# Graph convolution of a graph network in products of rounded halves, with the counts rounded once and at most five rows gathered for their rest

## The reference

```python
def _gcn_conv(x, src, dst, W, b, n):
    h = x @ W
    deg = jax.ops.segment_sum(jnp.ones_like(dst, dtype=x.dtype), dst, num_segments=n)
    dis = jnp.where(deg > 0, jax.lax.rsqrt(jnp.maximum(deg, 1.0)), 0.0)
    norm = dis[src] * dis[dst]
    msg = h[src] * norm[:, None]
    out = jax.ops.segment_sum(msg, dst, num_segments=n)
    return out + b

x = x + blocks(relu(layernorm(x)), ...)          # the four blocks
h = jnp.maximum(_layernorm(x, axis=-1), 0.0)
h = relu(_gcn_conv(h, src, dst, W1, b1, n))      # with one more loop on each node
x = x + _gcn_conv(h, src, dst, W2, b2, n)
```

## Time and profile before

| | |
|---|---|
| median of 3 runs | 1967.62 us (1966.53 to 1967.95) |
| the profiled execution | 1967.23 us |
| its span, first to last instruction | 1965.5 us |
| PE busy | 1890.2 us, 96% of the span |
| DVE, ACT, POOL busy | 1373.7, 783.1, 449.4 us |
| mean granted TensorE clock | 0.994 of full speed |

### The profile page before, as it was taken

One profiled execution on the slowest core, in us unless ns is written; L12 is line 12 of the kernel. 1 busy time (PEld: TensorE's weight loads), 2 busy tenths in 40 slices (PEclk: granted clock), 3 DMA queues, 4 the chain that ended last, 5 costly groups with the idle time before them and its releaser, 6 DMA issues. The chain is left out here.

```text
span 1965.5 us, 33581 instructions
## 1 busy us (share of the span) xinstructions
PE 1890.2 (96%) x11664; PEld 1562.3 (79%) x11664; DVE 1373.7 (70%) x2830; ACT 783.1 (40%) x1528; POOL 449.4 (23%) x525
## 2 busy tenths in 40 slices
PE   6988999999999999999999999999999999899999
PEld 3545888999889899988898999889989998775443
DVE  7887658888875588888657888885498888730111
ACT  1332455555432355544224555542255554330000
POOL 1000243112342422213325111252241113500000
PEclk9999999999999999999999999999999999999999
DMA  4112553111300112112102110301121106110001
GB/s 136 47 43 44 154 160 105 37 37 29 117 33 22 58 39 63 34 39 83 40 25 66 54 36 25 121 1 43 48 58 37 36 26 177 42 37 0 0 21 31
DMA packets 50719, 108.36 MB, mean 55 GB/s; under 512 B 18143, under 2 KB 18195, under 8 KB 50608
## 3 DMA queue, kind: packets, MB, share of 16 engines
q1 hardware_dynamic: 50608, 106.87, 18.5%
HBM read 83.60 MB, written 23.25 MB: 54 GB/s over the span
## 5 line engine op out<-in xcount | busy, mean ns | idle before, releaser
L785 ACT ACTIVATE PT<-ps 125x500 fp32r<-125x500 f32 (+1 forms) x480 | 214.2, 520 | 324.3 <-PE ps L1596 324.3
L1503 PE MATMUL ps<-PT,V 125*128 125x250 f32 x2400 | 313.2, 284 | 1.6 <-DVE PT L1173 1.6
L1503 PE MATMUL ps<-kT,qg 128*125 128x512 f32 (+1 forms) x1440 | 302.5, 354 | 6.8 <-DVE nmx L1157 5.5
L1503 PEld LDWEIGHTS ps<-PT,V 125*128 125x128 f32 x2400 | 289.6, 190 | 2.9 <-DVE PT L1173 2.9
L1503 PEld LDWEIGHTS ps<-kT,qg 128*125 128x125 f32 x1440 | 246.0, 186 | 57.3 <-issue 9.6
L1173 DVE TENSOR_TENSOR PT<-ps,PT 125x500 fp32r<-125x500 f32 (+1 forms) x480 | 253.0, 582 | 2.1 <-ACT PT L785 1.8
L1157 DVE CUSTOM_DVE_ANT_0 SB<-ps,bt 125x1250 f32<-125x1250 f32 x140 | 203.9, 1457 | 47.0 <-PE ps L1503 44.6
L1596 PE MATMUL ps<-ident,pbuf 125*125 125x125 f32 x1600 | 202.4, 274 | 13.6 <-DVE pbuf L1166 13.6
L1596 PEld LDWEIGHTS ps<-ident,pbuf 125*125 125x125 f32 x1600 | 187.3, 189 | 16.6 <-DVE pbuf L1166 15.9
L779 ACT ACTIVATE pbuf<-SB,nmx 125x1250 f32<-125x1250 f32 x140 | 188.1, 1344 | 8.7 <-DVE nmx L1157 7.4
L1166 DVE TENSOR_SCALAR pbuf<-pbuf,rden 125x1250 f32<-125x1250 f32 x160 | 149.8, 936 | 5.6
(11 more groups left out here) (194 smaller groups left out, 2715.4 us busy)
## 6 DMA issues: line engine op xcount, KB each, us to landing
bt<-edge_bias_scratch SPq DMA_DIRECT2D x40, 546.9 KB
q_scratch<-qc SPq DMA_DIRECT2D x16, 500.0 KB, 2.6
qc<-q_scratch SPq DMA_DIRECT2D x16, 500.0 KB, 4.8
counts_scratch<-cblk SPq DMA_DIRECT2D x10, 546.9 KB
c_rows<-counts_scratch SPq DMA_DIRECT2D x10, 546.9 KB
edge_bias_scratch<-b_rows SPq DMA_DIRECT2D x10, 546.9 KB
counts<-counts_scratch SPq DMA_DIRECT2D x10, 546.9 KB
wm<-in_L_gnn_wo_dram SPq DMA_DIRECT2D x4, 1024.0 KB, 8.4
```

Of the source, the lines that this page charges most:

```text
L785: sc.activation(PT[:, h % 2, 0, a:b, u * T:(u + 1) * T], ps_T[0:T, i, 0:(b - a) * T].rearrange("p (t n) -> p t n", n=T), ACT.Copy).then_in ...
L1503: e = mm(out_, lhs(a), rhs(b), start=start and i == 0, stop=stop and i == 2)
```

## The change

1. The counts of each tile are written once more as float32r (`whole`), in place, by an ACT copy that also sums each row (`whole_out`). The kernel takes whole numbers up to 4096 as exact in it. The rows of W1's product are kept as two halves, `hsH` (ACT, `rows_out`) and `hsL` (DVE, `rows_low`).
2. Both aggregations take two float32r matmuls (`hsH` and `hsL` with `whole`) for one in float32. The W2 product takes three, by `product`: W2 is split into `W2h` (ACT) and `W2l` (DVE), the first aggregation's result into `aggH` (ACT) and `aggL` (DVE).
3. A row of counts whose sum reaches 4096 has a rest that `whole` drops. At most five rows can. Ten small matmuls (`tri`, `ones` with `flag`) number them, a selection matrix `sel` is built, ten matmuls read their row numbers, POOL gathers these rows of the counts from DRAM by an indirect DMA, their rest `rest5` is computed on DVE, and one matmul of 5 rows per output piece adds it (`add_rest`, `last_rest`). This always runs, whatever the counts.
4. x is added by POOL ahead of the MLP bias for chunks 2 to 4, and by DVE for chunks 0 and 1, after `front_mod` in chunks 2 and 3. `front_relu(0)` moves on DVE from the last MLP chunk to the one before it. POOL adds the self loops and writes `diags`. The first four `whole_out` stand in ACT's order in the last two MLP chunks, the other six in the last stage.
5. The spread of `dis` (ones with `diags`) is done after the third chunk of the last stage.

The core of the diff:

```diff
@@ gpsimd, layer and what follows it
                     if c + 1 < NC:
+                        if last and c:
+                            add_x(c + 1)
                         mlp_bias(l, c + 1)
-                    if last and c in (1, 2):
-                        add_x(c - 1)
+                    if last and c >= 2:
+                        for t in (2 * c - 4, 2 * c - 3):
+                            self_loop(t)
...
-            for c in range(2, NC):
-                add_x(c)
+            pool.wait_ge(s["wa"], AHEAD + 3 * L + 1)
             g.memset(ones[:, :], 1.0).then_inc(s["onesr"], 1)
...
+            for t in range(NT):
+                e = g.tensor_scalar(diags[:, t * T:(t + 1) * T], ident[0:T, 0:T], dis[:, t:t + 1], None, ALU.mult)
...
+            for t in range(6, NT):
+                self_loop(t)
+            pool.wait_ge(s["g_wide"], 5)
+            g.indirect_dma_start(wide_x[:, :], None, counts_dram[:, :],
+                                 bass.IndirectOffsetOnAxis(ap=idx[:, 0:1], axis=0)).then_inc(s["g_gath"], 16)
@@ scalar
+            def whole_out(t):
+                act.wait_ge(s["g_eye"], t + 1)
+                sc.activation(whole[t][:, :], counts[t][:, :], ACT.Copy, accum_out=hsum[:, t:t + 1]).then_inc(s["g_H"], 1)
...
                     for c in range(NC):
                         if c:
                             yT_out(f2 + c)
-                        rsqrt0(f2 + c + 1)
-                        if c == NC - 1:
+                        if c < NC - 1:
+                            rsqrt0(f2 + c + 1)
+                        else:
                             front_relu(0)
                         h_out(l, c)
...
+                        if c == NC - 2:
+                            rsqrt0(f2 + NC)
+                        if c >= NC - 2:
+                            for t in range(2 * c - 6, 2 * c - 4):
+                                whole_out(t)
...
                 for u in range(2):
-                    act.wait_ge(s["g_hs_mm"], 2 * c + u + 1)
-                    sc.activation(hs[:, 2 * c + u, :], ps_q[0:T, u, :], ACT.Copy, scale=dis[:, 2 * c + u:2 * c + u + 1]).then_inc(s["g_hs"], 1)
+                    rows_out(2 * c + u, u, 2 * c + u)
+                if c == 0:
+                    for t in (4, 5):
+                        whole_out(t)
+                else:
+                    whole_out(5 + c)
+                if c == 1:
...
+                    sc.activation(W2h[:, :, :], W2[:, :, :], ACT.Copy).then_inc(s["g_w2h"], 1)
@@ vector
                     front_mod(f2 + c + 1)
+                    if last and c in (2, 3):
+                        add_x(c - 2)
+                    if last and c == 3:
+                        front_relu(0)
                     mlp_add(l, c, yT, weights)
 
                 dve.wait_ge(s["zC"], AHEAD + f + 2 * (NC - 1))
                 if last:
-                    front_relu(0)
                     front_relu(1)
...
-                yT_low(fg + c, yT2 if c % 2 else yT)
+                yT_low(fg + c, yTb if c % 2 else yT)
+                for u in range(2):
+                    rows_low(2 * (c - 1) + u, u, 2 * (c - 1) + u)
@@ tensor
-            for j in range(KD):
...
-                    for m in range(NT):
-                        e = mm(psf[:, o + a:o + b], hs[:, m, j * 128:(j + 1) * 128], counts[m][:, a:b],
-                               start=(m == 0), stop=(m == NT - 1))
+            def gather_rows(j, p):
...
+                for m in range(NT):
+                    if j == 0 and p == 0:
+                        pe.wait_ge(s["g_H"], m + 1)
+                        pe.wait_ge(s["g_hs"], m + 1)
+                    for i, half in enumerate((hsH, hsL)):
+                        mm(psf[:, o + a:o + b], half[:, m, j * 128:(j + 1) * 128], whole[m][:, a:b], start=m == 0 and i == 0,
+                           stop=False, skip_group_check=True)
+            pe.wait_ge(s["g_disb"], 1)
+            gather_rows(0, 0)
...
+            gather_rows(0, 1)
...
+            gather_rows(0, 2)
+            wide_rows(6)
...
+            pe.wait_ge(s["g_b5"], 2)
+            gather_rows(1, 0)
+            gather_rows(1, 1)
+            pe.wait_ge(s["g_h5e"], 1)
+            pe.wait_ge(s["g_b5"], 5)
+            for p in range(3):
+                add_rest(0, p)
...
-                    e = mm(ps_q[0:T, t % 2, :], aggT[:, k, t * T:(t + 1) * T], W2[:, k, :], start=(k == 0), stop=(k == KD - 1))
+                    e = product(ps_q[0:T, t % 2, :], lambda i: (aggH, aggL)[i][:, k, t * T:(t + 1) * T],
+                                lambda i: (W2h, W2l)[i][:, k, :], k == 0, k == KD - 1)
...
-                for m in range(NT):
-                    e = mm(ps[0:T, t % 2, :], counts[m][:, t * T:(t + 1) * T], hs[:, m, :], start=(m == 0), stop=(m == NT - 1))
+            last_rows(0)
+            wide_rows(2)
+            last_rows(1)
```

More of the change, by code:

```diff
@@ L180, in build @@
-        hs = place("hs", [T, NT, D], F32, r_wm)
+        r_counts = ([r_kv + 4 * KD * D + 5024 * i for i in range(3)] + [r_kv + 4 * 8 * KD * D + 5024 * i for i in range(3)]
+                    + [r_kv + 4 * 3 * KD * D + 5024 * i for i in range(4)])
+        assert r_counts[2] + 4 * N <= r_kv + 4 * 3 * KD * D and r_counts[5] + 4 * N <= kv_end
+        counts = [place(f"counts{t}", [T, N], F32, r_counts[t]) for t in range(NT)]
+        whole = [place(f"whole{t}", [T, N], F32R, r_counts[t]) for t in range(NT)]
@@ new lines, in _ @@
+            dve.wait_ge(s["g_wide"], 2)
+            dve.wait_ge(s["g_wide"], 1)
+            for r in range(WIDE):
+                e = v.scalar_tensor_tensor(out=sel[:, :, r], in0=ps[0:T, 6, 0:NT], scalar=float(r), in1=flag[:, :],
+                                           op0=ALU.is_equal, op1=ALU.mult)
+            e.then_inc(s["g_wide"], 1)
+            dve.wait_ge(s["g_wide"], 4)
+            v.tensor_copy(idx[:, :], ps[0:WIDE, 7, 0:1]).then_inc(s["g_wide"], 1)
+            dve.wait_ge(s["g_h5"], 1)
@@ new lines, in add_rest, with wide_rows @@
+            def add_rest(j, p):
+                a, b = COLS[p]
+                o = 1536 * (j % 2)
+                mm(psf[:, o + a:o + b], hs5[0][:, j * 128:(j + 1) * 128], rest5[:, a:b], start=False, stop=True,
+                   skip_group_check=True).then_inc(s["g_ag"], 1)
+            def wide_rows(bank):
+                for m in range(NT):
+                    e = mm(ps[0:WIDE, bank, :], sel[:, m, :], hsH[:, m, :], start=m == 0, stop=m == NT - 1)
+                e.then_inc(s["g_h5"], 1)
@@ new lines, in _ @@
+            pe.wait_ge(s["g_disb"], 1)
+            gather_rows(0, 0)
+            pe.wait_ge(s["g_tri"], 2)
+            pe.wait_ge(s["g_wide"], 1)
+            mm(ps[0:T, 6, 0:NT], tri[:, :], flag[:, :], start=True, stop=False, skip_group_check=True)
+            for k in range(1, NT):
+                e = mm(ps[0:T, 6, k:NT], ones[:, 0:T], flag[:, 0:NT - k], start=False, stop=k == NT - 1, skip_group_check=True)
+            e.then_inc(s["g_wide"], 1)
+            gather_rows(0, 1)
+            pe.wait_ge(s["g_row"], 2)
@@ new lines, in _ @@
+            pe.wait_ge(s["g_wide"], 3)
+            for m in range(NT):
+                e = mm(ps[0:WIDE, 7, 0:2], sel[:, m, :], rowid[:, m, :], start=m == 0, stop=m == NT - 1)
+            e.then_inc(s["g_wide"], 1)
+            gather_rows(0, 2)
+            wide_rows(6)
+            for p, (a, b) in enumerate(PIECES):
+                for m in range(a, b):
+                    e = mm(ps[0:WIDE, 3 + p, (m - a) * T:(m - a + 1) * T], sel[:, m, :].bitcast(F32), ident[0:T, 0:T], start=True, stop=True)
@@ new lines, in _ @@
+            e.then_inc(s["g_b5"], 1)
+            pe.wait_ge(s["g_b5"], 2)
[5 more added lines that the diff above has]
+                add_rest(0, p)
+            gather_rows(1, 2)
+            for p in range(3):
+                add_rest(1, p)
+            for j in range(2, KD):
+                for p in range(3):
+                    gather_rows(j, p)
+                    add_rest(j, p)
```

205 lines of the change are left out of this document (149 added, 56 removed).

## The result

| | before | after |
|---|---|---|
| median of the runs | 1967.78 us (1966.53 to 1968.07) | 1912.67 us (1909.78 to 1913.6) |
| the profiled execution | 1967.23 us | 1912.56 us |
| its span | 1965.5 us | 1910.8 us |

The ratio is 0.9719, 95% interval 0.9702 to 0.9735: 55 us less, where 60.5 were forecast. The time lies inside the forecast range of 1899 to 1915, 5.7 us above the predicted 1907 and just above the prediction's own bounds for its forecast as summed, 1902 to 1912.

What follows compares the result with a forecast made beforehand. PE, busy 96% of the span, was taken as the bound. Terms -78.0 + 8.7 + 1.8 + 4.5 - 1.4 + 2.6 + 0 + 1.3 = -60.5 us on 1967.23 gave 1906.7, stated as 1907; 8-in-10 range 1899 to 1915.

Steps and rivals of the forecast that it cites:

- the front: Stretch from the first nodes matmuls of MLP chunk 0 that wait for hT to aggregation 1; forecast +7.0 us.
- second rival: Search for rows with a rest holds PE up, by slow gathered rows or dearer tiny matmuls (+7.3); 1911 to 1920; chance 0.15.
- first rival: Last MLP chunks: transposes not held up (wait under 2 us) or clock does not fall; 1901 or 1899; chance 0.2.
- first wait: PE's new wait before features of chunk 4, the last MLP chunk, for yT: +4.5 us.
- Half products: Both aggregations and W2's product: float32r matmuls of 512 columns at 0.236 us; -35.5, -6.1 and -36.4, rest included.
- third rival: Half products cost what a float32 record costs, 0.43 us and not 0.236; kernel slower, 2015 us; chance 0.02.
- The rest: Added matmuls for the rest in both aggregations, priced like other float32r matmuls; 2.3 us in aggregation 1.
- The search: New PE work finding rows with a rest, +8.7 us; waits +1.8 for gather_rows, 0.8 in aggregation 2; DMA hidden.
- The clock and the third wait: Half clock after the 4.5 us wait, +2.6 us; the 1.82 us wait before nodes of chunk 4 shrinks, -1.4.
- The second wait: 3.78 us before transposes of the last stage's second chunk, with its clock fall: unchanged, 0, bounds -2.5 and +2.5.
- The five chunks: Last stage: ACT's count copies eat its slack, W2's copy does not fit and partly reaches PE; +1.3 us, between 0 and 5.
- The rival that the norm comes no sooner: Norm computed a chunk sooner, but PE meets it no sooner; within the forecast, worth 3.8 + 2.6 at most, 1901.

Runs made afterwards that it cites:

- e5: The changed kernel without the search for rows with a rest and without the rest's matmuls, so part of the computation is left out; 1889.87 us.
- e6: The changed kernel with the product with W2 in plain float32 matmuls again, 40 for 120; 1916.99 us.
- e1: The changed kernel with the rest's operands held in 125 rows, 120 of them zeros, instead of 5; 1903.85 us.
- e2: The changed kernel with ACT's copies of counts 0 and 1 ahead of the first norm's Ln and Exp; 1910.68 us.
- e9: The changed kernel with ACT's copies of counts 2 and 3 moved behind the first yT of the last stage; 1908.22 us.
- e3: The changed kernel with the norm of the last stage's first chunk back behind the last MLP chunk, on DVE and ACT; 1904.85 us.
- e7: e3 with x of the first two chunks added on POOL instead of DVE; 1904.05 us.
- e11: e10 with the first norm and DVE's adds of x put back where the change has them; 1903.56 us.
- e4: The changed kernel with DVE's adds of x and first norm right behind mlp_add, and chunk 4's yT copy ahead of that norm's Ln and Exp on ACT; 1906.05 us.
- e10: e8 with ACT's copies of counts from 2 on spread behind the halves of hs, and W2's copy behind the last chunk; 1894.21 us.
- e8: e7 and e1 together, against the changed kernel; 1898.65 us.

## Why the prediction was right, and where it was off

The mechanism was right: PE's matmuls got cheaper one for one, and the new work ahead of the last stage took some of it back. That the time came out within 5.7 us is in part luck, since the aggregations came 5.9 us dearer and the front 1.5 cheaper, out of several misses both ways. By its number alone the time also lies in the second rival's band (1911 to 1920), but neither of that rival's causes was met: the gathered rows were there in time, and the numbering cost 0.8 us more, not 7.3. The first rival is out: the first wait is 4.52 us, with the clock down.

- **Half products.** Right. The steps are 0.231 to 0.233 us where 0.236 was used. Aggregation 1 without its rest is 46.1 us (e5), which is the forecast's 160 x 0.236 + 80 x 0.104; aggregation 2 without it 39.7 shorter than before, where 38.8 follows from the forecast; W2 6.1 (e6). The third rival, 0.43 us a matmul, is out. By the four passes that the Trainium skill gives a true FP32 matmul (FP8 and Floating Point Precision, TensorE Precision Notes) it would be 25% of 0.86, an estimate of 0.215, and the three parts 11 us less (the prediction says 10); the runs decide, 0.231 to 0.233, or 27%.
- **The rest.** The step that failed. It was priced as 2.3 + 2.4 us, the same matmul with fewer rows. Its changes of rows cost 6.1 us more (e1), about the 5.9 by which the aggregations came dearer. The prediction had no rival for it.
- **The search.** Forecast 8.7, with waits of 1.8 and 0.8; measured 9.4, with waits of 1.7 and 0.6. The numbering took 2.1 for 1.3: its smallest float32 records cost 0.105 us each, and not the 0.063 of a bfloat16 one. The gathered rows are hidden: the DMA took 3.2 us from issue to landing where 13.5 were taken as free; issued at 1775.58, the rows were first read by DVE at 1783.60. Of the port between GpSimd's DMA and DVE the Trainium skill warns (SBUF — State Buffer, SBUF: two separate sides). No run here tests it: DVE was idle, waiting for PE, from 1775.25 to 1779.76.
- **The first wait.** Forecast 4.5, measured 4.52, with the causes wrongly weighed, so the closeness is luck. 2.7 us were put down to ACT's copies; with them out of the way 3.46 remain (e2). The working left out what DVE has to do itself between the Exp and `yT_low`, five small steps and the first add of `mlp_add`, 1.94 us beside the copies, and its two adds of x took 2.59 where 1.38 and 0.7 were taken.
- **Chunk 3.** Not forecast: 1.38 us, from the same adds of x a chunk sooner, where POOL was busy too. The stretch of DVE's two adds beside POOL was taken as 0.7 us; it was 1.2 at chunk 4 and 2.7 at chunk 3.
- **The clock and the third wait.** The fall behind the first wait was forecast at 2.6, and took 7.38 - 5.71 = 1.7 in after, and 8.49 - 5.71 = 2.8 in e5. The wait before `nodes` of chunk 4 went from 1.82 to 0.51 us; -1.4 was forecast.
- **The second wait.** Forecast at 3.78, measured 2.08. The copies do make it, as the working said (e9 takes them away: 0.33), but DVE's five steps beside POOL's `diags` took 0.16 to 0.33 us each and not half: 1.3 us in all for 5.4 before, and with 2.5 for the two copies that gives 3.78 - 4.1 + 2.5 = 2.2. With its slow clock it went from 12.8 us of wait and work to 10.1 (1734.64 - 1726.60 + 2.08), 2.7 less: a little past the cheap bound of 2.5.
- **The five chunks.** Forecast +1.3; from the transposes at 1734.64 to aggregation 1 it is 28.6 us for 27.0: +1.5. The size came out, the cause did not. W2 was to be what does not fit; but the two waits, 0.70 for ACT's `pbuf` behind copies of counts and 0.38 for DVE's `hsL`, end at 1743.39, ahead of W2's copy, and PE has no wait behind it until the search's at 1783.62. Timeline of ACT in after:

```profile
1744.16 1.91 ACT L981 ACTIVATE W2h<-W 128x2048 fp32r<-128x2048 f32 x1
```

- **The rival that the norm comes no sooner**, which the forecast took in, was right: the second wait is 2.08 with the early norm and 2.09 without (e3). What the early norm costs was summed as 4.5 - 1.4 + 2.6 = 5.7. Measured on the front, the early norm alone costs 6.4 (e3), with DVE's adds of x 8.2 (e7), and both together 6.8 where ACT's copies are spread (e11).

Open is why the clock fell behind the numbering in the profiles of e2, e3 and e4 alone, how often it does so in after, and why it fell behind the second wait in after and not in e5. Each kernel has one profile, so the shares of the clock above are those of single executions.

## What to carry to other kernels

Ask of a cheap extra matmul what it does to its neighbours' loads: one with 5 rows among those of 125 cost 0.63 us (its own 0.23 and 0.40 more), and padded with zeros 0.23. Work that is moved to be ready sooner is worth nothing unless the wait that PE meets is released by it; look for what stands ahead of it on the engine that it is moved to, and what stands behind it there. Off the critical engine, copies without a deadline belong into the places where that engine already waits: moving eight of them, and W2's, took 2.4 us off the front (e10 against e8), with no instruction less.
